# A recurrent stage whose PE, ScalarE and VectorE work is reordered: later and earlier copies, a wider centring matmul, one operation for h

## The reference, cut to what matters

```
x = x + slstm_layer(ln(x, ln1_w))         # conv over time, gates, recurrence, norm per head
x = x + ffn(ln(x, ln2_w))                 # (gelu(u[:, :336]) * u[:, 336:]) @ wd, u = x @ wu

def step(carry, wx_t):                    # once per token, h is the state of 4 heads of 64
    raw = wx_t + einsum('bhd,hdgo->bhgo', h, rk) + b
    ir, fr, zr, og = raw[:, :, 0], raw[:, :, 1], raw[:, :, 2], raw[:, :, 3]
    lfm = m + log_sigmoid(fr);  mn = maximum(ir, lfm)
    ig = exp(ir - mn);  fg = exp(lfm - mn)
    cn = fg * c + ig * tanh(zr);  nn = fg * n + ig
    hn = sigmoid(og) * cn / nn
y = (y - mean) * rsqrt(var + EPS) * gn_w  # per head of 64 features
```

## Time and profile before

| what | value |
|---|---|
| median of 3 runs | 4049.7 us (4048.94 to 4052.33) |
| the profiled execution | 4048.4 us, of which the span of the core 4046.7 us |
| PE busy | 3876.7 us (96%) |
| DVE busy | 3681.0 us (91%) |
| ACT busy | 3256.1 us (80%) |
| POOL busy | 2211.6 us (55%) |
| mean granted clock of PE | 0.989 of full speed |

### The profile page before, as it was taken

One profiled execution on the slowest core, in us unless ns is written; L12 is line 12 of the kernel. 1 busy time (PEld: TensorE's weight loads), 2 busy tenths in 40 slices (PEclk: granted clock), 3 DMA queues, 4 the chain that ended last, 5 costly groups with the idle time before them and its releaser, 6 DMA issues. The chain is left out here.

```text
span 4046.7 us, 170045 instructions
## 1 busy us (share of the span) xinstructions
PE 3876.7 (96%) x70778; PEld 2189.0 (54%) x70778; DVE 3681.0 (91%) x10771; ACT 3256.1 (80%) x6720; POOL 2211.6 (55%) x2425
## 2 busy tenths in 40 slices
PE   6999999999999999999999998799999999999997
PEld 3555555555555555555555554466666666666664
DVE  7999999999999999999999998788888888888886
ACT  4999999999999999999999998466666666666665
POOL 3666666666666666666666666444344443444443
PEclk9999999999999999999999999899999999999998
DMA  2000111000000000000000000000000001000000
GB/s 77 21 23 23 48 54 51 21 23 23 21 23 23 21 23 23 21 23 23 21 23 23 21 23 24 17 22 23 31 24 23 23 22 33 23 22 22 26 21 9
DMA packets 101034, 105.27 MB, mean 26 GB/s; under 512 B 17536, under 2 KB 96032, under 8 KB 99768
## 3 DMA queue, kind: packets, MB, share of 16 engines
q1 hardware_dynamic: 100264, 94.39, 8.0%
HBM read 48.68 MB, written 17.69 MB: 16 GB/s over the span
## 5 line engine op out<-in xcount | busy, mean ns | idle before, releaser
L596 POOL TENSOR_TENSOR conv_products<-normed_features,conv_taps_by_token 128x256 f32<-128x256 f32 (+1 forms) x852 | 780.4, 916 | 609.7 <-DVE convolved_features L549 358.5
L309 PE MATMUL banks<-up_centred,after_cell_features 128*32 128x336 f32 x9088 | 759.6, 452 | 0.0
L786 POOL TENSOR_TENSOR exps_of_both_halves<-scores 128x256 f32<-128x256 f32 x512 | 419.1, 842 | 619.9 <-ACT scores L1042 614.7
L285 PE MATMUL banks<-down,hidden_features 112*32 112x256 f32 x6816 | 427.5, 384 | 0.0
L365 ACT ACT_TABLE_LOAD x284 | 364.4, 1283 | 52.7 <-PE banks L265 47.8
L586 POOL TENSOR_TENSOR conv_partial_sums<-conv_products,conv_partial_sums 128x512 f32<-128x512 f32 x284 | 364.8, 1285 | 66.6 <-DVEq L485 44.4
L1042 ACT ACTIVATE scores<-scores 128x512 f32<-128x512 f32 x512 | 305.4, 626 | 116.3 <-DVE scores L1190 115.4
L309 PEld LDWEIGHTS banks<-up_centred,after_cell_features 128*32 128x32 f32 x9088 | 237.2, 109 | 270.6 <-issue 270.6
L386 ACT ACT_TABLE_LOAD x284 | 364.4, 1283 | 5.0
L1190 DVE SCALAR_TENSOR_TENSOR scores<-banks,score_top 128x512 f32<-128x512 f32 x512 | 327.7, 681 | 27.0 <-PE banks L872 26.4
L258 PE MATMUL banks<-recurrent_weights,h_features 64*32 64x256 f32 x9088 | 311.7, 383 | 1.4 <-ACT h_features L358 1.4
(11 more groups left out here) (215 smaller groups left out, 10055.6 us busy)
## 6 DMA issues: line engine op xcount, KB each, us to landing
layer_inputs<-layer_outputs SPq DMA_DIRECT2D x284, 96.0 KB, 2.0
layer_inputs<-in_x SPq DMA_DIRECT2D x285, 32.0 KB, 1.8
x_scratch<-layer_outputs SPq DMA_DIRECT2D x284, 32.0 KB, 1.8
x_tokens<-in_x SPq DMA_DIRECT2D x32, 256.0 KB, 3.1
context_features<-in_ctx SPq DMA_DIRECT2D x32, 256.0 KB, 3.8
layers_out<-x_scratch SPq DMA_DIRECT2D x32, 256.0 KB, 2.9
out<-result SPq DMA_DIRECT2D x64, 128.0 KB, 1.8
up_centred<-in_ff_up SPq DMA_DIRECT2D x1, 2688.0 KB
```

What stands on the lines that cost most here:

```text
L285: mm = nc.tensor.matmul(bank[group(l), FD, 0:D], hidt[:, i, group(l)], down[:, l, i, :], start=i == 0, stop=i == UTILES - 1, skip_group_ch ...
L309: mm = nc.tensor.matmul(bank[group(l), b, 0:UP], xmt[:, n, group(l)], up[:, l, n, at:at + UP], start=n == 0, stop=n == HALF - 1, skip_grou ...
L596: nc.gpsimd.tensor_tensor(prod[:, i:i + n], xnt[:, j % NRING].rearrange("p n t -> p (n t)")[:, None, :].broadcast_to([P, n, HALF * P]), ta ...
L786: nc.gpsimd.tensor_tensor(psum[:, i % RING, :], pr[:, i % RING, 0:S], pr[:, i % RING, S:2 * S], ALU.add).then_inc(halves_added, 1)
```

## The change

Five edits, all in `slstm`:

- **h by one operation.** DVE wrote h in two halves of 128 columns in an order that puts the heads of one half side by side; now it writes all 256 columns at once in the order of the heads. So the transpose of h becomes four products of 64 columns of h with the identity (matmul, no longer `transpose`), and the statistics read plain slices.
- **Centring by whole rows.** centre_and_scale becomes 128 x 128 per layer and half, with the other head's block zero, and `centred` 8 matmuls on 128 rows with 128 columns instead of 16 on 64 rows with 64 columns. Its matrix is loaded by two DMAs, two memsets clear the rest, and the operation that scales it is twice as wide. The rows of the bias are kept in a buffer of the second stage until that is loaded.
- **ACT: gated rows' features copied in the next step.** The copy of hidden_features moves from the end of a step to after the ln of the growth in the next one.
- **ACT: normed rows' features ahead of the gelu.** The copy of normed_features and the gelu change places.
- **DVE: two operations earlier.** cell_out moves from behind minus_decay_logit to behind normed, and after_cell from behind layer_outputs to behind v.

```diff
@@ slstm
-    gnc = sb("centre_and_scale", [P, LAYERS, HALF, DH])
+    gnc = sb("centre_and_scale", [P, LAYERS, HALF, 2, DH])
...
             def centred(j):
                 for n in range(HALF):
                     for l in range(LAYERS):
-                        for odd in range(2):
-                            r = slice(DH * odd, DH * odd + DH)
-                            at = UP + n * DH
-                            mm = nc.tensor.matmul(bank[group(l), UPG + odd, at:at + DH], ht[r, n, group(l)], gnc[r, l, n, :],
-                                                  start=n == 0, stop=True, skip_group_check=True)
+                        mm = nc.tensor.matmul(bank[group(l), UPG + n, UP:UP + P], ht[:, n, group(l)],
+                                              gnc[:, l, n].rearrange("p r d -> p (r d)"), start=True, stop=True, skip_group_check=True)
                 mm.then_inc(cen_ready, 1)
...
                 if j > 0:
-                    pe.wait_ge(h_done, 2 * j)
-                transposes(FD, D, h, ht_ready)
+                    pe.wait_ge(h_done, j)
+                for n in range(HALF):
+                    for odd in range(2):
+                        i = odd * HALF + n
+                        mm = nc.tensor.matmul(bank[DH * odd:DH * odd + DH, FD, D + n * P:D + (n + 1) * P], h[:, i * DH:(i + 1) * DH], ident[:],
+                                              start=True, stop=True, skip_group_check=True)
+                mm.then_inc(ht_ready, 1)
...
                 nc.scalar.activation(bank[:, FD, D:], spb[:], ACT.Ln, bias=1.0).then_inc(sp_step, 1)
+                if j > 0:
+                    act.wait_ge(hidt_ready, j)
+                    copy(both(hidt[:]), bank[0:UT, CV, 0:UTILES * P], hidt_copied)
                 act.wait_ge(gn_mv, HEADS * (j + 1))
...
+                act.wait_ge(xnt_ready, j + 1)
+                copy(both(xnt[:, j % NRING]), bank[:, CV, 0:D], xnt_copied)
                 act.wait_ge(yn_done, j + 1)
                 nc.scalar.activation(gl[:], bank[:, UPG, 0:UP], ACT.Gelu, scale=rs[:, HEADS:HEADS + 1]).then_inc(gelu_done, 1)
-                act.wait_ge(xnt_ready, j + 1)
-                copy(both(xnt[:, j % NRING]), bank[:, CV, 0:D], xnt_copied)
...
-                act.wait_ge(hidt_ready, j + 1)
-                copy(both(hidt[:]), bank[0:UT, CV, 0:UTILES * P], hidt_copied)
...
                 dve.wait_ge(o_done, j + 1)
                 dve.wait_ge(cell_step, 3 * j + 3)
-                for n in range(HALF):
-                    nc.vector.scalar_tensor_tensor(out=h[:, n * P:(n + 1) * P].rearrange("p (r d) -> p r d", r=2), in0=heads_of(ot[:], n),
-                                                   scalar=1.0, in1=heads_of(half_r[:], n), op0=ALU.add,
-                                                   op1=ALU.mult).then_inc(h_done, 1)
+                nc.vector.scalar_tensor_tensor(out=h[:], in0=ot[:], scalar=1.0, in1=half_r[:], op0=ALU.add,
+                                               op1=ALU.mult).then_inc(h_done, 1)
```

More of the change, by code:

```diff
@@ L30 @@
 ROW_SCALE = 16.0
-UP_SCALED = 34
+UP_SCALED = 36
 EPS = 1e-5
@@ L120, in slstm @@
     BIAS = 2 * 512
-    rows = sb("bias_rows", [3 * LAYERS, BIAS])
-    rows_rest = sb("bias_rows_rest", [3 * LAYERS, BIAS])
+    lent = kept["sums"][:].rearrange("p a n -> p (a n)")
+    rows, rows_rest = lent[0:3 * LAYERS, 0:BIAS], lent[0:3 * LAYERS, BIAS:2 * BIAS]
+    pieces = kept["pieces"]
     rows_hi, rows_mid, rows_lo = (sb("bias_hi", [3 * LAYERS, BIAS], F16), sb("bias_mid", [3 * LAYERS, BIAS], F16),
@@ L205, in group @@
         return slice(32 * l, 32 * l + 32)
-    LOADS = 10
+    LOADS = 11
     FIRST_PIECE = 40
@@ L214, in _ @@
             for dst, src in ((wg, a["gate_w"]), (rk, a["rker"]), (up, a["ff_up"]), (down, a["ff_down"]), (conv_w, a["conv_w"]), (conv_b, a["conv_b"]),
-                             (ln1, a["ln1"]), (ln2, a["ln2"]), (gnc, a["gn_w"]), (rows, a["bias"])):
+                             (ln1, a["ln1"]), (ln2, a["ln2"]), (rows, a["bias"])):
                 sy.dma_start(dst[:], src).then_inc(w_loaded, DMA)
+            for odd in range(2):
+                r = slice(DH * odd, DH * odd + DH)
+                sy.dma_start(gnc[r, :, :, odd], a["gn_w"][r]).then_inc(w_loaded, DMA)
             sy.wait_ge(zeroed, 1)
@@ L412, in _ @@
                 nc.vector.memset(buf[:], val).then_inc(w_step, 1)
+                n += 1
+            for odd in range(2):
+                nc.vector.memset(gnc[DH * odd:DH * odd + DH, :, :, 1 - odd], 0.0).then_inc(w_step, 1)
                 n += 1
@@ L452, in _ @@
             n += TAPS + 2 * (TAPS + 1)
-            f_ = rows[:, 0:1024].rearrange("p (h g d) -> p h g d", h=HEADS, g=GATES)[:, :, 1, :]
+            f_ = rows[:, 0:BIAS].rearrange("p (h g d) -> p h g d", h=HEADS, g=GATES)[:, :, 1, :]
             nc.vector.tensor_scalar(f_, f_, -1.0, None, ALU.mult).then_inc(bias_made, 1)
@@ L505, in _ @@
                                         ALU.subtract, ALU.mult).then_inc(xn_done, 1)
+                dve.wait_ge(cen_ready, j + 1)
+                nc.vector.tensor_tensor(yn[:].rearrange("p (r n d) -> p r n d", r=2, n=HALF),
+                                        bank[:, UPG:UPG + 2, UP:UP + P].rearrange("p n (r d) -> p r n d", r=2),
+                                        rs[:, 0:HEADS].rearrange("p (r n) -> p r n", r=2)[:, :, :, None].broadcast_to(
+                                            [P, 2, HALF, DH]), ALU.mult).then_inc(yn_done, 1)
                 dve.wait_ge(f_step, 2 * j + 1)
@@ L508, in _ @@
                 nc.vector.tensor_tensor(heads(v[:]), heads(ls[:]), gate(j, 0), ALU.subtract).then_inc(decay_step, 1)
+                dve.wait_ge(yn_done, j + 1)
+                nc.vector.tensor_tensor(xm[:, j % MRING], yn[:], xr[:, (j - 2) % XRING, :], ALU.add).then_inc(xm_done, 1)
                 dve.wait_ge(f_step, 2 * j + 2)
```

22 lines of the change are left out of this document (7 added, 15 removed).

## The result

| | median, us | range | runs |
|---|---|---|---|
| before | 4049.32 | 4047.9 to 4052.33 | 4 |
| after | 4091.93 | 4090.92 to 4093.48 | 4 |

The ratio is 1.0105 (95% interval 1.0087 to 1.0122): slower by 42.6 us where the prediction said 82. The direction and the range held. The size did not, and the experiments show that the reason given for the slowdown was not the cause; that the direction came out right was luck.

What follows compares the result with a forecast made beforehand. A ring of DVE and ACT (8.66 us) was taken to bound the kernel before, one of DVE and POOL (8.95) after. 284 x 0.29 = 82, +1, gave 4131 us, in a range of 4055 to 4150.

Steps and rivals of the forecast that it cites:

- a ring of DVE and POOL: After the change, DVE and POOL alone set the step: 8.95 us, +0.29 a step.
- The sum of 4.81 + 3.82: Kernel before: DVE's cell operation to log_rstd, then ACT to tanh z; claimed as the ring that sets the 8.66 us step.
- ACT then runs on, through its table load: Kernel before, ACT from log_rstd through gelu and normed copy to tanh z's end, claimed without a wait: 3.82 us.
- four rounds for 64-column tiles: Transpose of h on PE: 8 records run in pairs, four rounds instead of two, +0.22 us.
- +0.20 for the cell operation: With the normed copy ahead of the gelu, hidden and the cell's first operation on DVE come 0.20 us later.
- PE isn't in the ring: On the normed copy: PE gets normed_features 0.44 us earlier, claimed not to matter to the step.
- gap g on POOL: Wait before POOL's product after its preceding operation L590 ends: taken as 0.18 us, bounds 0.08 and 0.21.
- 0.29 a step: Forecast slowdown of each first-stage step, from 8.66 to 8.95 us.
- The chain through PE, 8.63: From one transpose of h to the next after the change: 8.63 us with h products paired, under 8.95.
- Rival 1: DVE and POOL alternate in winning the port: mean step 8.74, 4073 us, at most 4090; chance 0.22.
- Rivals 2 to 4: No change, 4043 to 4050 us (0.10); faster, 4013 us (0.10); slower still, 4164 us (0.08).
- rival 4: PE becomes the bound because the h products don't overlap: step 9.06, +0.40, 4164 us; chance 0.08.

Runs made afterwards that it cites:

- e8: The kernel before with the normed copy ahead of the gelu (and loads and bias rows set up like the kernel after): 4016.93 us, ratio 0.9921.
- e7: The kernel after with h in halves, the old centring and DVE's old order, leaving only ACT's two moved copies: 4016.48 us, ratio 0.992.
- e10: The kernel before with only h by one operation and its four products on PE: 4108.97 us, ratio 1.0147.
- e3: The kernel after with h back in two halves, turned by two full transposes: 4062.37 us, ratio 1.0034.
- e4: The kernel after with the centring back to 32 matmuls of 64x64 in tiles of 64x32: 4074.54 us, ratio 1.0065.
- e9: The kernel before with only DVE's new order, cell_out and after_cell earlier: 4037.26 us, ratio 0.9971.
- e12: The kernel after with the gelu back ahead of the normed copy: 4100.9 us, ratio 1.0127.
- e11: The kernel before with only the hidden copy moved to ACT's next step: 4048.96 us, ratio 1.0000.
- e6: The kernel after with h in halves and the old centring, DVE's new order kept: 4061.66 us, ratio 1.0031.
- e2: The kernel before with POOL's first product waiting until the cell's first operation on DVE is done: 4046.95 us, ratio 0.9997.
- e1: The kernel after with POOL's first product waiting until the cell's first operation on DVE is done: 4090.41 us, ratio 1.0105.

## Why the prediction was right or wrong

The two rings, in us a step:

| part | ring through softplus | ring through normed | run |
|---|---|---|---|
| kernel before | 8.658 | (8.53) | |
| normed copy ahead of the gelu | 8.51 | the step is 8.534 | e8, e7 |
| h by one, 8 records | +0.22 | +0.219 | e10, e3 |
| centring by whole rows | 0 | +0.057 | e4 |
| cell_out early on DVE | -0.029, while the gelu is first | 0 | e9, e12 |
| hidden copy next step | 0 | 0 | e11 |

(8.51: where the recurrence releases the softplus in e8, the load ends 0.039 before the copy, and 0.012 is enough.) 8.534 + 0.219 + 0.057 = 8.810, against 8.807 measured; 0.057 is the sum of the places on PE in e4, whose step moved by 0.055. The change is a gain of 0.12 and a loss of 0.28, both on PE and ACT.

The measured time lies in the stated range and on the side that was forecast, but by luck: the forecast slowdown came from a ring of DVE and POOL that does not set the step, the measured one from a term on PE that the prediction worked out and then did not count.

- **What bounds the kernel: wrong, and the root of the rest.** The sum of 4.81 + 3.82 gave 8.66 because log_rstd starts when DVE's statistics end. But a chain is a ring only if each next link is tight too. The step that failed is "ACT then runs on, through its table load": the link from rstd to the softplus has 0.1 us of slack, hidden because the recurrence on PE releases the softplus at the same hundredth. e9 brought log_rstd 0.35 earlier, and the softplus did not move. The gelu was not released by the load either, as the prediction took it, but by DVE's cell_out (0.093 after its end in nearly every step before).
- **h by one operation.** On DVE 0.43 where 0.42 was forecast (-0.07, of no use). On PE the estimate of four rounds for 64-column tiles, +0.22, was right, and it is the largest term of the result. The prediction put it on a chain of 8.63 beside the ring, and so at nothing.
- **Normed copy ahead of the gelu: right on DVE, wrong in sign for the kernel.** +0.20 for the cell operation was measured as +0.21. What counts is that PE's transpose of after_cell no longer waits for the copy: -0.125. "PE isn't in the ring" was the mistaken sentence.
- **Hidden copy.** 0, right (e11).
- **cell_out and after_cell earlier.** DVE's times were right: minus_decay_logit ends 2.28 after normed starts (1517.52 to 1519.80; forecast 2.29), or 2.44 in the other kind of step, where cell_out waits for PE's centring. The gap g on POOL was not: L597 ends at 1511.60 and the product starts at 1511.83, 0.23, and it is 0.229 to 0.231 in 277 to 279 of the 284 steps in each kernel in which the product follows that addition at once (after, e3, e4, e6, e9, e12). The forecast was 0.18 with 0.21 as its upper bound, and 0.23 is the value at which the prediction called itself wrong. POOL still leads by 0.11 in every second step, since PE holds the gelu, and so the cell, back. The port does as forecast where POOL is first. But all this lies on DVE and POOL, which are slack in the kernel after. It costs something only once PE is faster: 45 us between e6 and e7. The prediction's 0.29 a step was worked out for a ring that wasn't the longest. (Its range by g ends at 8.98 us, which gives 4140, not 4143.)
- **Centring.** Taken as 0 between -0.1 and +0.2; measured +0.057, 16 us. The matmuls themselves got shorter (0.518 to 0.461 from start to start). The recurrence ahead of them grew by 0.136 in the same measure though its own records end when they did (1.09 long, both): PE loses that time where the tiles change from 64x32 to 128x32.
- **The chain through PE, 8.63.** It let the normed copy start as early as the gelu had. It left out that PE must first get from the transpose of h through recurrence, centring and down projection to the transpose of normed: 3.91 before (1507.02 to 1510.93), 4.18 after (1514.70 to 1518.88). With the 0.10 behind it the copy starts 4.72 after the transpose of h, where the chain had it at 1.61 + 2.72 + 0.22 = 4.55 (to log_rstd, from there to the place that the gelu had, and h). That is the missing 0.18.
- **Rival 1** foresaw the alternation of L541 (661 ns in the mean against 786 before) and came nearest in time (4073, at most 4090). Its reason for the size, a mean of long and short steps, was wrong for this kernel: all steps are equal. It fits e3 and e6. Rivals 2 to 4 fell: DVE does not win every step, and the h products do overlap in pairs. What rival 4 said of the bound, though, was nearer than the forecast: PE's idle time in the stretch of the earlier trace rows fell from 44 to 10 us, where the prediction's signs had it grow.

The best kernel found keeps one edit of five: the normed copy ahead of the gelu, 4017 us (e8; with the hidden copy moved too, e7, the same).

## What to carry to other kernels

A sum of durations that equals the step proves no ring. Go round once more and ask of every start which *other* engine ended just before it, above all where two ends fall within 0.1 us of each other. The cheapest proof is an experiment that takes time out of one link: if the step doesn't move, that link has slack. But look in its trace whether the time is really gone (in e2 most of it came back at h). And price an edit on every ring that is within its own size of the longest: here three rings lay within 0.13 us before, and within 0.03 in e8, so each edit's cost depended on which others were in.

## What the runs showed of the hardware

- **Who gets the port, and from which lead.** Going through all steps of the kernel after, e3 and e6: where POOL's product was ahead by 24 ns or more and still running, it won, and the DVE operation ended about 0.29 after it; at leads up to 0.12 us it so lasted 0.90 to 0.99 instead of 0.42. Where POOL was ahead by 16 or 17 ns (four steps) or DVE ahead by anything, DVE won. The Trainium skill, SBUF — State Buffer, "Who interferes with whom", says that the first to issue holds the pair for a whole instruction; these runs agree, but for leads under 24 ns by the starts in the trace. Who wins decides nothing for the kernel's time if neither is on the ring (e1).
- **A start on POOL behind several waits takes 0.230 us** from the end of the operation before it, within 0.001 in nearly every step (the row of 1511.83), where one with a single releaser takes 0.08 to 0.09. The trace doesn't say how the waits share it.
- **Tiles of 64 columns run in pairs.** The four products for h are 8 records and take 0.587 us to the next group; two full transposes are 2 records and take 0.368. In the kernel after the records start in pairs, the second 0.007 behind the first, and the last pairs 0.109 apart. The Trainium skill, TensorEngine Tiling (Array Packing), "Restrictions", says that column tiling turns off the transpose mode for FP32 input, which would account for two records to a product instead of one; the runs show the count, not the reason.
- **A change of tile shape: about 0.14 us.** The recurrence's place on PE is 0.888 us long with the centring in its own shape (64x32) behind it and 1.024 with 128x32 (e4), its records and their number being the same. The Trainium skill, TensorEngine Tiling (Array Packing), "Key Properties", says that a change of mode drains the engine, without a price. The runs fit that; they don't show that it is the drain.
